# An audio tower with routed experts on one core: no key projection, other load queues, new orders

## The reference

```python
h = tok(x)                       # compress conv 128->64, silu, conv of width 3, silu, expand 64->128,
                                 # + x, layer norm, feed-forward 128->64->128 with gelu, + , layer norm,
                                 # running max over 3 tokens: 373 tokens are left
h = h + attn(layernorm(h))       # q = (z Wq + bq) / sqrt(128); k = z Wk + bk
                                 # softmax(q k^T) z, z the normalised h
h = h + moe(layernorm(h))        # gate: relu(z gw1 + gb1) gw2 + gb2, softmax, best 2 of 8 experts,
                                 # softmax of the two weights; expert e: gelu(z we1[e] + be1[e]) we2[e] + be2[e]
```

## Time and profile before

| | |
|---|---|
| median of 3 runs | 247.51 us (247.3 to 248.34) |
| the profiled execution | 247.55 us |
| its span, first to last instruction | 245.6 us |
| mean granted TensorE clock | 0.993 |
| TensorE busy | 234.1 us (95%) |
| VectorE busy | 156.2 us (64%) |
| ScalarE busy | 144.4 us (59%) |
| GpSimd busy | 114.3 us (47%) |

### The profile page before, as it was taken

The page is one execution under the profiler, slowest core; times in us unless marked ns, Lnnn a source line. Parts: engine busy times, 40 slices in busy tenths (PEclk is TensorE's granted clock), DMA queues, the critical chain, the costliest instruction groups (busy, mean ns, idle before and its releaser), DMA issues.

```text
span 245.6 us, 5357 instructions
## 1 busy us (share of the span) xinstructions
PE 234.1 (95%) x1651; PEld 185.3 (75%) x1651; DVE 156.2 (64%) x663; ACT 144.4 (59%) x292; POOL 114.3 (47%) x185
## 2 busy tenths in 40 slices
...
GB/s 150 242 249 308 371 411 414 410 412 415 215 0 4 0 0 4 1 3 31 32 42 77 43 44 93 102 107 264 263 313 205 44 68 61 74 45 107 73 32 65
...
## 3 DMA queue, kind: packets, MB, share of 16 engines
...
HBM read 10.28 MB, written 21.28 MB: 128 GB/s over the span
## 4 chain that ended last, share of the span: by engine, by line
PE 80%; DVE 12%; issue 3%; ACTq 2%; ACT 2%; DVEq 0%
PE PS L1148 16%; PE PS L1141 16%; PE PS L1173 7%; PE PS L1164 7%; PE PS L1066 6%; PE PS L1084 5%; PE PS L956 3%; PE PS L1073 3%; DVE stat L672 2%; PE PS L1056 2%; PE PS L1060 2%; PE PS L1157 2%; PE PS L1031 2%; PE PS L1033 2%; PE PS L985 1%
## 5 line engine op out<-in xcount | busy, mean ns | idle before, releaser
L640 ACT ACTIVATE gd<-PS,bias 128x373 f32<-128x373 f32 x64 | 35.0, 572 | 28.9 <-PE PS L1141 27.0
L1148 PEld LDWEIGHTS PS<-w_all,gd 128*125 128x125 f32 x384 | 44.8, 187 | 4.2 <-ACT gd L640 0.7
L1148 PE MATMUL PS<-w_all,gd 128*125 128x128 f32 x384 | 46.3, 273 | 0.0
L1141 PE MATMUL PS<-xt_sb,w_all 128*128 128x373 f32 x128 | 46.0, 482 | 0.1
L513 POOL DMA_INDIRECT yg<-ys,pos_x x24 | 29.3, 1219 | 19.6 <-issue 19.3
L883 DVE SCALAR_TENSOR_TENSOR x_sb<-PS,comb,x_sb 125x128 f32<-125x128 f32 x84 | 24.3, 347 | 17.4 <-PE PS L1148 16.4
L467 POOL TENSOR_TENSOR ve<-mv,eps 125x3 f32<-125x3 f32 x32 | 6.2, 194 | 57.8 <-DVE mv L676 57.4
L492 POOL DMA_INDIRECT xs<-xn,pos_x x24 | 29.0, 1207 | 7.9 <-issue 6.7
L1141 PEld LDWEIGHTS PS<-xt_sb,w_all 128*128 128x128 f32 x128 | 21.4, 190 | 10.9 <-issue 4.3
L469 POOL TENSOR_TENSOR rstd<-ve,mhalf 125x3 f32<-125x3 f32 x32 | 27.5, 860 | 2.5
L1084 PEld LDWEIGHTS PS<-xn,prob_t 125*125 125x125 f32 (+1 forms) x144 | 16.8, 187 | 1.6 <-issue 0.7
...
## 6 DMA issues: line engine op xcount, KB each, us to landing
...
```

Source lines behind the costliest of these rows:

```text
L640: act.activation(gd[:, k % GD, c, 0:TP], of("D1", n)[:, 0:TP], ACT.Gelu, bias=bias128[:, 2 + k % E * HC + c:3 + k % E * HC + c]).then_inc( ...
L1141: pe.matmul(f[:, 0:TP], w_all[:, k % E, c * 128:(c + 1) * 128], x32[:, DENSE[k // E], 0:TP], start=True, stop=True).then_inc(S["D1"], 1)
L1148: last = pe.matmul(f[0:P, j * D:(j + 1) * D], gd[:, n % GD, c, OFF[j]:OFF[j] + P], w_all[:, n % E, H + c * D:H + (c + 1) * D], start=(c == ...
```

## The change

- The key projection `bk` and its tile `k_t` are gone. A piece `ft` transposes Wk and Wq, VectorE scales and shifts them, and `fn` multiplies them to one 128x128 matrix and one column for the bias (`nqk`). `bq` multiplies z by this matrix, and the scores multiply its result by `xn_t` itself. The copy of `b1` adds 1.0, which the shift of the weights accounts for.
- ScalarE issues five loads (two of `bias64`, two of `wm_d`, `row_be`). x of the first two pairs and `rows6` go to SyncE's queue, Wk, Wq and `bias128` to GpSimd's. ScalarE's first activation, which loads its table, waits for the identity instead of `bias64`, and stands ahead of the load of `row_be`.
- The copy of `hr` has its own name `hv` and is on VectorE for sequences 0, 2, 4 and 5; seven `xT` copies, `g1.1`, `g1.3`, `ct.1` and `ct.3` go to VectorE.
- All orders are new. There are nine filler pieces with 51 matmuls instead of eight with 23. `fin.3` is the last piece of VectorE.
- Semaphores of evictions are counted by the rank on their engine instead of by parity; all scatters share one semaphore, the gathers two.

The core of the diff, the orders cut to the parts spoken of:

```diff
-w.0:1 a1.0:0 w.1:1 a2.0:0 a2.1:1 a1.1:2 cb.0:0 a3.0:1 a3.1:3 a2.2:2 a2.3:0 a1.2:4 bf.0:0 a3.2:1 a3.3:2 a2.4:3
...
+w.0:0 a1.0:0 w.1:1 a2.0:0 a2.1:1 ft.0:2 a1.1:3 a3.0:1 a3.1:0 a2.2:3 a2.3:4 cb.0:2 w.2:5 a1.2:1 a3.2:4 a3.3:3
+bf.0:2 a1.3:0 a4.0:5 fn.0:6 w.3:1 a4.1:1 a2.4:2 a2.5:7 a5.0:1 w.4:5 a6.0:1 a6.1:3 a2.6:0 a2.7:7 a4.2:2 a3.4:4
+a3.5:5 a4.3:0 a7.0:1 w.5:2 a7.1:3 w.6:2 a3.6:7 a3.7:3 a5.1:0 hr.0:5 w.7:1 a4.4:1 hr.1:4 a6.2:5 a4.5:6 a6.3:1
+b1.0:6 a5.2:4 bq.0:6 w.8:0 b1.1:0 sc0.0:6 sc1.0:4 bq.1:0 sc2.0:5 a7.2:7 sc0.1:0 sc1.1:6 pt0.0:5 pt1.0:4 pt2.0:2
...
+T.11:0 h1.7:5 L1.10:7 L2.8:3 L2.9:4 g1.3:5
+D1.33:1 T.12:0 T.13:2 D1.34:7 D2.14:0 L1.11:6 T.14:3 L2.10:1 L1.12:2 g2.3:6 T.15:0 L1.13:4 D1.35:6 T.16:3
+L2.11:0 L2.12:1 L1.14:2 L1.15:4 T.17:3 L2.13:0 L1.16:3 T.18:2 L2.14:5 L2.15:2 L1.17:4 L2.16:3 L1.18:5 L2.17:7
+D1.36:6 L2.18:5 ct.2:3 D2.15:4 bd.2:3 D1.37:2 D1.38:6 D1.39:7 D2.16:2 D1.40:0 D1.41:5 D1.42:6 D2.17:4 ct.3:3
...
 DVE_ORDER
-da.24 da.25 fin.2 da.26 da.27 da.28 da.29 fin.3 da.30 da.31
+ft.0 a3.0 a3.1 cb.0 l1.0 l1.1 bf.0 a4.0 a3.2 a3.3 a6.0 a6.1 l2.0 a3.4 a3.5 mp.0 l1.4 hv.0 hr.0 fn.0 hr.1 l3.0
...
+bd.3 fin.1 da.22 da.23 da.24 da.25 fin.2 da.26 da.27 da.28 da.29 da.30 da.31 fin.3
 ACT_ORDER
+a1.0 a2.0 a2.1 a1.1 a2.2 a2.3 a1.2 a4.1 a5.0 a2.4 a2.5 a1.3 l1.2 l1.3 a2.6 a4.2 l2.1 a7.0 a7.1 a2.7 a4.3 a5.1
...
+dg.17 g3.2 b1.7 dg.18 dg.19 sc0.6 dg.20 bq.7 sc1.6 sc2.6 sc0.7 dg.21 dg.22 sc1.7 dg.23 dg.24 sc2.7 dg.25 dg.26
...
-WARM = (6, 2, 2, 5, 1, 2, 3, 2)
+WARM = (11, 6, 6, 2, 6, 6, 10, 2, 2)
...
             load_xt(0)
             for s in range(2):
                 sp.dma_start(we_d[HALF[s], :], we).then_inc(S["we"], 16)
+            load_x(sp, 0)
             load_xt(1)
+            sp.dma_start(rows6[:], b_rows[:, 0:6 * D].rearrange("o (r d) -> (o r) d", d=D)).then_inc(S["rows6"], 16)
+            load_x(sp, 1)
...
+            for dst, src in ((wk_sb, wk), (wq_sb, wq), (bias128, b128)):
+                pool.dma_start(dst[:], src).then_inc(S["wqk"], 16)
...
             for s in range(2):
+                act.dma_start(bias64[HALF[s], 0:4], b64).then_inc(S["b64"], 16)
+            for s in range(2):
                 act.dma_start(wm_d[HALF[s], :, :], wm).then_inc(S["wm"], 16)
-            for s in range(2):
-                act.dma_start(bias64[HALF[s], 0:4], b64).then_inc(S["b64"], 16)
-            load_x(act, 0)
+            act.wait_ge(S["ident"], 4)
+            act.activation(tiny[:], ident[0:1, 0:1], ACT.Silu)
             act.dma_start(row_be[:], b_rows[:, 0:D].broadcast_to([P, D])).then_inc(S["rows"], 16)
-            act.dma_start(rows6[:], b_rows[:, 0:6 * D].rearrange("o (r d) -> (o r) d", d=D)).then_inc(S["rows6"], 16)
-            load_x(act, 1)
+            act.wait_ge(S["b64"], 32)
...
+                if name == "ft":
+                    dve.wait_ge(S["wqk"], 16 * 3)
+                    wait(dve, "ft", 1)
+                    f = of("ft", 0)
+                    link(dve.tensor_reduce(sums[:], f[:, 0:2 * D].rearrange("e (w i) -> e w i", w=2), AX.X, ALU.add))
+                    dve.tensor_scalar(wqt[:], f[:, D:2 * D], SCALE, None, ALU.mult)
+                    dve.tensor_scalar(shift[:, 1:2], sums[:, 1:2], bias128[:, 0:1], -SCALE, ALU.subtract, ALU.mult)
+                    link(dve.tensor_scalar(shift[:, 0:1], sums[:, 0:1], bias128[:, 1:2], -1.0 / D, ALU.subtract, ALU.mult))
+                    dve.tensor_scalar(wkt[:], f[:, 0:D], shift[:, 0:1], None, ALU.add).then_inc(S["fd"], 1)
...
+                    pe.matmul(f[:, 0:D], wqt[:], wkt[:], start=True, stop=True)
+                    pe.matmul(f[:, D:D + 1], wkt[:], shift[:, 1:2], start=True, stop=True).then_inc(S["ft"], 1)
...
-                    pe.matmul(f[:, 0:TP], wq_sb[:], xn_t[:, s, :], start=True, stop=True).then_inc(S["qp"], 1)
-                if name == "bk":
-                    wait_nth(pe, "xnt", n)
-                    f = claim(name, n, nth("k", n))
-                    pe.matmul(f[:, 0:TP], wk_sb[:], xn_t[:, s, :], start=True, stop=True).then_inc(S["kp"], 1)
+                    pe.matmul(f[:, 0:TP], nqk[:, 0:D], xn_t[:, s, :], start=True, stop=True).then_inc(S["qp"], 1)
...
-                    pe.matmul(f[0:P, 0:TP], q_t[:, s, OFF[j]:OFF[j] + P], k_t[:, s, :], start=True, stop=True)\
+                    pe.matmul(f[0:P, 0:TP], q_t[:, s, OFF[j]:OFF[j] + P], xn_t[:, s, :], start=True, stop=True)\
```

More of the change, by code:

```diff
@@ L60 @@
 XN4 = 6
+assert all(n - XN4 not in SPARSE for n in range(B))
 ZN = 8
 PE_ORDER = """
-w.0:1 a1.0:0 w.1:1 a2.0:0 a2.1:1 a1.1:2 cb.0:0 a3.0:1 a3.1:3 a2.2:2 a2.3:0 a1.2:4 bf.0:0 a3.2:1 a3.3:2 a2.4:3
-a2.5:4 a4.0:0 a1.3:5 a3.4:4 w.2:6 a2.6:5 a2.7:1 a4.1:0 a3.5:3 a5.0:2 a4.2:5 a3.6:1 w.3:6 a6.0:2 a6.1:4 a4.3:5
-a3.7:3 a5.1:5 a4.4:0 a4.5:6 a7.0:5 a6.2:0 a7.1:1 a6.3:4 a5.2:1 w.4:7 a4.6:3 w.5:7 hr.0:1 hr.1:6 a4.7:5 w.6:7
-a7.2:0 a6.4:3 a7.3:0 a6.5:4 b1.0:5 a5.3:6 b1.1:0 bq.0:1 bk.0:6 bq.1:0 bk.1:1 sc0.0:6 sc1.0:0 sc2.0:1 sc0.1:5
@@ L70 @@
[L70 to L84, removed]
@@ new lines @@
+pt2.3:5 hr.5:1 D1.5:4 at.3:5 ct.0:0 h1.2:6 D1.6:4 D1.7:0 bd.0:2 a7.6:5 D1.8:3 b1.4:1 D2.0:6 ct.1:1 h1.3:2 bq.4:5
+b1.5:4 g1.1:6 sc0.4:5 sc1.4:0 g2.1:6 sc2.4:7 D1.9:4 bq.5:1 D2.1:6 a7.7:1 sc0.5:5 D2.2:0 pt0.4:7 pt1.4:2 sc1.5:3
+rk.1:1 D1.10:4 sc2.5:6 pt2.4:7 D1.11:2 D1.12:5 pt0.5:6 at.4:7 pt1.5:6 hr.6:1 pt2.5:4 D2.3:3 at.5:4 D1.13:0
+h1.4:5 hr.7:1 D1.14:7 bd.1:0 D1.15:4 D2.4:6 h1.5:2 D2.5:5 g1.2:2 D1.16:3 b1.6:7 g2.2:2 D1.17:1 D1.18:7 bq.6:6
+D1.19:2 b1.7:5 sc0.6:6 D2.6:3 sc1.6:1 D2.7:5 rk.2:7 D1.20:4 bq.7:2 sc2.6:6 D2.8:7 sc0.7:2 sc1.7:4 D1.21:5
@@ L99 @@
+yv.1 da.13 yv.2 xT.5 yv.3 xT.7 yv.4 yv.5 l4.7 yv.6 xT.11 xT.12 yv.7 yv.8 g1.3 yv.9 da.14 g2.3 xT.15 yv.10 yv.11
+g3.3 yv.12 yv.13 yv.14 cw.3 yv.15 yv.16 yv.17 yv.18 bd.2 da.15 da.16 ct.3 da.17 da.18 da.19 da.20 fin.0 da.21
+bd.3 fin.1 da.22 da.23 da.24 da.25 fin.2 da.26 da.27 da.28 da.29 da.30 da.31 fin.3
 """
 ACT_ORDER = """
-a1.0 a2.0 a2.1 a1.1 a2.2 a2.3 a1.2 a2.4 a2.5 a4.0 a1.3 l1.2 a2.6 a2.7 a5.0 l1.4 a4.3 a5.1 a4.4 l2.1 a7.0 a4.5
-a7.1 l1.6 a5.2 l1.7 hr.0 l2.2 hr.1 a4.7 a7.2 a5.3 b1.1 bq.0 bk.0 bq.1 bk.1 sc0.0 sc1.0 sc2.0 sc0.1 sc1.1 pt1.0
```

225 lines of the change are left out of this document (123 added, 102 removed).

## The result

| | before | after |
|---|---|---|
| median of 5 runs each | 248.34 us (247.3 to 248.62) | 249.98 us (249.63 to 250.14) |
| ratio after/before, 95% | | 1.0075 [1.0058, 1.0093] |
| profiled execution, span | 247.55, 245.6 us | 249.94, 248.2 us |
| start of L2.18 | 195.0 | 199.9 |
| from there to the end | 50.6 | 48.3 |

The change makes the kernel slower by 0.75%, where I had forecast 243.8 us; the time lies above my range (240.0 to 248.2) as well. The cut at L2.18 says at once in which half: the tail is as forecast (48.3 against 48.6), and L2.18 comes 6.7 us later than the 193.2 of the sum.

What follows compares the result with a forecast made beforehand. TensorE's matmul stream was taken as the bound, VectorE and the gathers close behind. L2.18 at 195.07 - 0.7 (K, net) - 1.8 (start) + 0.6 (tables) = 193.2, plus 48.6 and 1.95: 243.8 us, range 240.0 to 248.2.

Steps and rivals of the forecast that it cites:

- the tail: From L2.18 to the end, fin.3 behind da.31: 48.6 us instead of 50.5, 1.9 of 3.8 us kept.
- the sum: L2.18 at 195.07 - 0.7 - 1.8 + 0.6 = 193.2; span 241.8; plus 1.95 around the span, 243.8 us.
- I take 0.6 (half a load), bounds 0 and 12.8: Ten more table loads on ScalarE: cover remains, so 0.6 us reaches the time, 12.8 at most.
- rival 2: ScalarE becomes the bound: ten more table loads delay evictions TensorE needs; 249.6 us with half reaching it; chance 0.08.
- None of TensorE's waits now follows a table load: In the kernel before, no wait of TensorE comes after a table load; used as support for the 0.6 us.
- The start, -1.8 forecast: Earlier table load and new load order: first residual add at 11.1, gain 1.8 us carried to L2.18, bounds 0 and 5.1.
- Whatever leaves the stream should leave the time, unless something stands close behind.: TensorE's matmul stream sets the time after its start; K's matmuls hold it 5.0 us, 0.7 net before L2.18.
- fillers cost nothing: 28 more filler matmuls on TensorE stand where it waits anyway: price 0 where they fit, 6.0 us at most.
- Rival 5: A table switch holds ScalarE twice as long as its load, with a drain: 256.0 us; chance 0.01.
- rivals 1 and 4: Rival 1: first part tightens fully, 240.5 us, chance 0.22. Rival 4: front's gain given back, tables 1.3, 246.3, chance 0.16.

Runs made afterwards that it cites:

- e4: The changed kernel with Tanh in place of all three Gelus, leaving two table loads; 244.71 us, ratio to before 0.9860.
- e5: The kernel before with Tanh in place of all three Gelus, leaving two table loads; 247.69 us, ratio to before 0.9993.
- e3: The changed kernel with the second pair's xt load issued ahead of the first pair's x on SyncE's queue; 249.34 us, ratio to before 1.0062.
- e2: The changed kernel with 12 filler matmuls instead of 51 (w.0 has 6 instead of 11); 253.59 us, ratio to before 1.0251.
- e8: The kernel before with every key projection matmul issued twice, 5.0 us more in the stream; 252.56 us, ratio to before 1.0189.
- e7: The kernel before with only the key projection taken out, loads and orders kept, ft and fn placed late; 249.65 us, ratio to before 1.0066.

## Why the prediction was wrong, step by step

- **The step that failed: "I take 0.6 (half a load), bounds 0 and 12.8".** The table loads of the new order cost 5.2 us more than those of the old (e4 against e5), 4.6 over the term. The count (24) and the place (six more between 82 and 150) were right, ScalarE's load there nearly so (50.5 forecast, 52.9 measured), and so was rival 2's mechanism, of which I said that it decides where more than 4.3 of the 12.8 us reach TensorE; I gave it 0.08. The error was to judge cover by the share of busy time over 68 us, "ScalarE is busy 45.1 of 67.9, so cover remains". Eight of the loads stand in 16.8 us in which ScalarE is busy 16.6. Three loads, the first of these eight among them, wait for the same row maximum as their Exp, with the idle time ahead of them. The sign that I named for rival 2, ScalarE's waits for TensorE vanishing between 82 and 150, would have missed it: ScalarE is still idle 15 of the 67.9 us.
- **"None of TensorE's waits now follows a table load".** That was misread. In before the first Gelu (L581, at 24.79) stands behind a load at 23.50, and TensorE waits for it:

```profile
PE PS L1031 <- ACT f L581: 0.5, 1, 0.5
```

  It cost nothing at the end: e5 has neither the load nor the wait, and hr.0 starts at 37.60 against 37.59. So the old order's loads were covered by their places, and that told nothing of ten loads at others.
- **The start, -1.8 forecast.** It failed too: the first residual add is at 13.61, 0.7 later than the 12.89 of the earlier trace rows, so this term is off by 2.5, and by e3 what is lost at the add stays to L2.18. Two of TensorE's rows in after:

```profile
1.72 5.03 PE L1000 MATMUL PS<-ident 128*128 128x128 f32 x22 [1.72 <-POOL ident L449]
...
11.87 0.85 PE L1006 MATMUL PS<-xt_sb,wc_p 128*64 128x375 f32 x4 [1.17 <-DMA xt_sb<-in_xt]
```

  w.0's 22 records run at 0.213 throughout, the 1.2 GHz level; I had full clock from 4.5 and w.0's end at 5.5. It ends at 6.75, a1.0 starts at 6.7. That alone cost little: in e2, with six fillers in w.0, a1.0 starts at 4.75 and a1.1 still only at 11.57. (Nor was TensorE idle from a1.0 to 8.45 in before, as I had it: fillers ran to 6.30, and the wait was 2.15 us.) What held the start is the transfer: xt of the second pair landed at 11.74 (8.43 in before): the first pair's x, issued ahead of it, cost far more than the 1.3 us of issue that I counted ("may take back some tenths"). With xt first (e3), x is the late one, and the add is at 12.88; which order of loads would give the 11.1 that I forecast, no run shows. Right in this part: the table load at 3.33, the first a2 in 1.21 us at full clock at 9.13, row_be no longer the late one on its queue (9.95 instead of 11.46).
- **"Whatever leaves the stream should leave the time, unless something stands close behind."** As a price of K's matmuls this was wrong: added work costs 4.6 of 5.0 (e8), removed work returns nothing (e7). In the sum it can't have hurt much: the new order has other pieces where K was (a5.3, D1.1 and a7.4 between bq.2 and sc0.2), the work before L2.18 fell by 0.8 as forecast, and without its table loads the new order takes 181.10 us from the first add to L2.18, where before takes 182.11.
- **Sum.** L2.18 at 199.9 against 193.2, 6.7 us late: 4.6 by the table loads (5.2 where 0.6 were taken) and 2.5 by the start, less 0.4 by which the rest came out better than forecast. The tail is 0.3 shorter than forecast: 6.4 of span in all, 241.8 to 248.2. That rival 2's 249.6 lies so near the measured 249.98 is luck in part: it had 6.4 for the tables, 1.2 too much, and kept the start's gain of 1.8, 2.5 too little.
- **Right: the tail.** da.31's last result leaves at 242.99 + 0.87, fin.3 follows and the stores after it:

```profile
242.99 0.87 DVE L915 SCALAR_TENSOR_TENSOR ob<-PS,comb,x_sb 125x128 f32<-125x128 f32 x3 [0.45 <-PE PS L1187]
243.77 0.87 DVE L957 SCALAR_TENSOR_TENSOR acc<-yg,w_top,x_sb 125x128 f32<-125x128 f32 x3
...
245.58 0.75 SPq L436 DMA_DIRECT2D out<-ob  x2
```

  That is t + 44.0 for da.31's end (44.1 forecast). Gathers stay 1.51 apart.
- **Right: fillers cost nothing** (e2: 39 of them are worth 3.6 us), and a table load costs its 1.28 us with no drain: after's 132.84 load is followed by its Exp at 134.13. Rival 5 is out by that. Of rivals 1 and 4, the first is contradicted by L2.18's start; the fourth (the front given back, tables 1.3) had the start nearly right (no gain) and the tables at a quarter of their size.
